# Feature arrays held twice, the staging array dropped, and the packs issued in slots 10 to 12

## What is computed

```python
f = b[:, :, ::2, ::2]                                   # 40 x 40 features
w = extract_patches(f, 3, 1)                            # 1600 patches of 64*3*3
wn = w / max(norm(w), 1e-4)
yi = einsum('bpd,bld->blp', w, wn) * mm                 # 1600 x 1600 scores
yi = softmax(yi * 10, axis=1) * mm
patches = einsum('blp,bld->bpd', yi, raw_w)             # raw_w: 4 x 4 patches of b
out = overlap_add(patches) / 4
```

## Time and profile before

| | us |
|---|---|
| median of three runs | 1486.64 (1485.1 to 1486.96) |
| the profiled execution | 1485.93 |
| its span | 1484.1 |

### The profile page before, as it was taken

How to read it: one execution, slowest core, us unless ns; L and a number is a source line. 1 busy time by engine, 2 the same in 40 slices (tenths; PEclk the granted TensorE clock), 3 DMA queues, 4 the chain that set the end, 5 groups by cost and what they waited for, 6 DMA issues and landing times.

```text
span 1484.1 us, 24228 instructions
## 1 busy us (share of the span) xinstructions
PE 1340.5 (90%) x7190; PEld 904.1 (61%) x7190; DVE 1195.3 (81%) x2830; ACT 853.7 (58%) x2233; POOL 47.6 (3%) x63
## 2 busy tenths in 40 slices
PE   4987999989999799998999899998999989999796
PEld 4765755667556675576656576566755666557343
DVE  4667889779888798878897878977888879888883
ACT  2667646656457564585555754666655755458431
POOL 1000000010000100001000000000000010000100
PEclk9997999999999999999999999999999999999999
DMA  5305462155622744137631556215462255412442
GB/s 101 45 1 133 108 130 70 51 150 116 127 61 65 172 101 109 52 85 165 122 93 34 130 128 136 78 44 143 119 124 72 62 143 113 111 51 83 129 137 57
DMA packets 181749, 146.57 MB, mean 99 GB/s; under 512 B 120114, under 2 KB 177522, under 8 KB 181618
## 3 DMA queue, kind: packets, MB, share of 16 engines
q1 hardware_dynamic: 181298, 144.04, 41.0%
q10 hardware_dynamic: 320, 0.99, 0.3%
HBM read 19.76 MB, written 13.11 MB: 22 GB/s over the span
## 4 chain that ended last, share of the span: by engine, by line
PE 32%; DVE 28%; SPq 11%; ACT 11%; issue 10%; DMA 7%; DVEq 0%; POOL 0%; ACTq 0%; POOLq 0%
PE psG L465 14%; PE psO L515 14%; DVE G L934 7%; DVE Z L967 5%; DVE G L874 4%; SPq L318 4%; DVE S L880 4%; DVE G L945 4%; ACT S L690 3%; ACT G L701 3%; SPq L299 3%; DMA HV<-LOHI 3%; PE psG L474 3%; ACT G L676 3%; DMA SH<-G 3%
## 5 line engine op out<-in xcount | busy, mean ns | idle before, releaser
L515 PE MATMUL psO<-Z,B 123*128 123x492 f32 (+2 forms) x1792 | 718.4, 530 | 38.5 <-DVE Z L967 25.2
L515 PEld LDWEIGHTS psO<-Z,B 123*128 123x128 f32 x1792 | 326.4, 194 | 238.1 <-issue 129.9
L465 PE MATMUL psG<-LH,HL 128*123 128x246 f16 (+2 forms) x2616 | 411.8, 287 | 38.2 <-DMA HV<-LOHI 28.7
L465 PEld LDWEIGHTS psG<-LH,HL 128*123 128x123 f16 x2616 | 280.5, 139 | 161.0 <-issue 96.7
L880 DVE CUSTOM_DVE_ANT_0 S<-G,RB 123x492 f32<-123x492 f32 (+1 forms) x448 | 269.1, 607 | 87.4 <-DVE G L874 55.0
L701 ACT ACTIVATE G<-G,nb 123x492 f32<-123x492 f32 (+1 forms) x448 | 267.0, 642 | 110.9 <-DVE G L934 110.4
L690 ACT ACTIVATE S<-S,nm 123x480 f32<-123x480 f32 (+3 forms) x560 | 307.3, 555 | 2.3 <-DVE nm L885 2.1
L945 DVE TENSOR_TENSOR G<-G,SH 123x492 f32<-123x492 f32 (+1 forms) x448 | 247.3, 591 | 54.2 <-DMA SH<-G 53.9
L934 DVE SCALAR_TENSOR_TENSOR G<-G,RA,psB 123x492 f32<-123x492 f32 (+1 forms) x448 | 270.1, 646 | 0.5 <-issue 0.5
L676 ACT ACTIVATE G<-psG 123x492 f32<-123x492 f32 (+3 forms) x256 | 120.1, 472 | 173.0 <-PE psG L465 92.5
L967 DVE TENSOR_TENSOR Z<-G 123x984 f32<-123x984 f32 (+2 forms) x192 | 197.3, 1028 | 0.6 <-PE psO L515 0.6
(11 more groups left out here) (83 smaller groups left out, 581.3 us busy)
## 6 DMA issues: line engine op xcount, KB each, us to landing
SH<-G SPq DMA_DIRECT2D x336, 214.8 KB
SH<-G SPq DMA_DIRECT2D x112, 89.2 KB
SH<-G SPq DMA_DIRECT2D x336, 19.2 KB
XP<-x SPq DMA_DIRECT2D x20, 280.0 KB, 5.9
XP<-mid SPq DMA_DIRECT2D x20, 280.0 KB, 5.3
HL<-LOHI SPq DMA_DIRECT2D x16, 246.5 KB, 3.5
mid<-OSB SPq DMA_DIRECT2D x48, 80.0 KB, 2.3
out<-OSB SPq DMA_DIRECT2D x48, 80.0 KB, 2.3
```

What stands on the lines that cost most here:

```text
L465: last = pe.matmul(psG[0:TW, bank, b0 * TW:b1 * TW], st[:, p:p + TW], mv[:, lo:lo + n], start=i == 0, stop=i == len(terms) - 1)
L515: last = pe.matmul(psO[:, b, 0:n], B[:, o:o + 128], Z[:, 2 * (s % 2) + j, 0:n], start=t == 0, stop=t == TILES - 1)
```

## The change

LH, HL, H1 and HV become two buffers each; unit w uses buffer w % 2. The staging array goes: `high_features` and `low_features` write straight into LH of the unit's buffer, whose two halves are the low and the high part. So the two LH packs go, and six are left (`N_F` = 6). They are issued in slots 10 (HL), 11 (H1) and 12 (HV), two each, behind the slot's copies, instead of all in slot 28 ahead of them. SP's wait for all scores of v in slot 28 becomes, in each of the three slots and for w of 2 and more, a wait for the scores of unit w - 2, which are long done. `high_features` waits for the same instead of for `f_in`. At the start DVE clears LH (twice the size) and no longer HL, H1 and HV, POOL no longer clears LOHI, and ACT's queue issues only the two HV packs.

```diff
-        HL = sb("HL", [128, FLEN], F16)
-        LH = sb("LH", [128, FLEN], F16)
-        H1 = sb("H1", [128, FLEN], F16)
-        HV = sb("HV", [128, FLEN], F16)
+        LH = sb("LH", [128, 2, FLEN], F16)
+        HL = sb("HL", [128, 2, FLEN], F16)
+        H1 = sb("H1", [128, 2, FLEN], F16)
+        HV = sb("HV", [128, 2, FLEN], F16)
-        LOHI = sb("LOHI", [128, FLEN], F16)
-        LS, HS = LOHI[0:64, :], LOHI[64:128, :]
-        CLEARED = 10
+        CLEARED = 6
-        N_F = 8
+        N_F = 6
+        def halves_of(w):
+            return LH[0:64, w % 2, :], LH[64:128, w % 2, :]
...
             def lay_out_features(w, which):
+                if w >= 2:
+                    sp.wait_ge(g_ready, (w - 1) * NB)
+                    sp.sem_inc(sp_gate, 1)
                 sp.wait_ge(h_made, 2 * (w + 1))
                 sp.sem_inc(sp_gate, 1)
                 sp.wait_ge(l_made, 2 * (w + 1))
-                for dst, src in packs(which):
+                for dst, src in packs(w, which):
                     sp.dma_start(dst, src).then_inc(f_in, 16)
...
-                    if s == SLOTS and w is not None:
-                        sp.wait_ge(g_ready, (v + 1) * NB)
-                        sp.sem_inc(sp_gate, 1)
-                        lay_out_features(w, ("HL", "LH", "H1", "HV"))
                     at = place(u, v, s + LEAD)
                     if at:
                         shift_pair(at)
                     at = place(u, v, s + 2)
                     if at and at[2] == 0:
                         shift_strip(at)
+                    if s in (10, 11, 12) and w is not None:
+                        lay_out_features(w, (("HL", "H1", "HV")[s - 10],))
...
-            def high_features(v, w):
+            def high_features(w):
                 act.wait_ge(feat_in, (w + 1) * STRIPS * 16)
-                if v is not None:
+                if w >= 2:
                     act.sem_inc(act_gate, 1)
-                    act.wait_ge(f_in, (v + 1) * N_F * 16)
+                    act.wait_ge(g_ready, (w - 1) * NB)
+                HS = halves_of(w)[1]
...
-            for tile, value in ((HL[:, :].bitcast(F32), 0.0), (LH[:, :].bitcast(F32), 0.0), (H1[:, :].bitcast(F32), 0.0),
-                                (HV[:, :].bitcast(F32), 0.0), (halves[0:64, 0:1], 1.0), ...
+            for tile, value in ((LH[:, :, :].bitcast(F32), 0.0), (halves[0:64, 0:1], 1.0), ...
...
-            pool.memset(LOHI[:, :].bitcast(F32), 0.0).then_inc(cleared, 1)
```

More of the change, by code:

```diff
@@ L244, in out_parts, with packs @@
                         yield a, j, at[0] - first, len(at), rows[at[0]] - 1 + a
-        def packs(which):
+        def halves_of(w):
+            return LH[0:64, w % 2, :], LH[64:128, w % 2, :]
+        def packs(w, which):
             n = FLEN
-            parts = {"HL": ((HL[0:64, :], HS), (HL[64:128, :], LS)), "LH": ((LH[0:64, :], LS), (LH[64:128, :], HS)),
-                     "H1": ((H1[0:64, :], HS), (H1[64:128, 0:n - 1], HS[:, 1:n])),
-                     "HV": ((HV[0:64, :], HS), (HV[64:128, 0:n - TW], HS[:, TW:n]))}
+            low, high = halves_of(w)
+            hl, h1, hv = (a[:, w % 2, :] for a in (HL, H1, HV))
+            parts = {"HL": ((hl[0:64, :], high), (hl[64:128, :], low)),
+                     "H1": ((h1[0:64, :], high), (h1[64:128, 0:n - 1], high[:, 1:n])),
+                     "HV": ((hv[0:64, :], high), (hv[64:128, 0:n - TW], high[:, TW:n]))}
             return [part for name in which for part in parts[name]]
@@ L457, in one_row, with products @@
                 return [(HL, LH, dy, dx) for dx in range(3)] + [(H1, H1, dy, 0), (HL, HL, dy, 2)]
-            def products(j, par, bank, b0, b1, terms):
+            def products(v, j, par, bank, b0, b1, terms):
                 s0 = S_CHUNKS[j // PAIRS][0]
@@ L464, in products @@
                     lo, p = (s0 + b0 + dy) * TW + dx, (t + dy) * TW + dx
-                    last = pe.matmul(psG[0:TW, bank, b0 * TW:b1 * TW], st[:, p:p + TW], mv[:, lo:lo + n],
+                    last = pe.matmul(psG[0:TW, bank, b0 * TW:b1 * TW], st[:, v % 2, p:p + TW], mv[:, v % 2, lo:lo + n],
                                      start=i == 0, stop=i == len(terms) - 1)
@@ L480, in even_tile @@
                     pe.wait_ge(p_copied, v * len(SHARED) + count(SHARED, j) - 1)
-                    products(j, 0, FREE, stored, w, SHARED_ROWS).then_inc(p_ready, 1)
+                    products(v, j, 0, FREE, stored, w, SHARED_ROWS).then_inc(p_ready, 1)
                 pe.wait_ge(even_read, v * SLOTS + j + 1)
@@ L488, in even_tile @@
                 if shared:
-                    last = products(j, 0, 0, stored, w, one_row(0))
+                    last = products(v, j, 0, 0, stored, w, one_row(0))
                 last.then_inc(g_ready, 1)
@@ L497, in odd_tile @@
                 if alone > stored:
-                    products(j, 1, 1, stored, alone, TERMS)
+                    products(v, j, 1, 1, stored, alone, TERMS)
                 if alone < w:
-                    last = products(j, 1, 1, alone, w, one_row(2))
+                    last = products(v, j, 1, 1, alone, w, one_row(2))
                 last.then_inc(g_ready, 1)
@@ L765, in body @@
                         if s == 5:
-                            high_features(v, w)
+                            high_features(w)
                         if s == 6:
@@ L778, in _ @@
             act.wait_ge(cleared, CLEARED)
-            high_features(None, 0)
+            high_features(0)
             squares(0)
@@ L783, in _ @@
             act.wait_ge(l_made, 2)
-            for dst, src in packs(("LH", "HV")):
+            for dst, src in packs(0, ("HV",)):
                 act.dma_start(dst, src).then_inc(f_in, 16)
@@ L802, in _ @@
             dve.sem_inc(dve_gate, 1)
-            for tile, value in ((HL[:, :].bitcast(F32), 0.0), (LH[:, :].bitcast(F32), 0.0), (H1[:, :].bitcast(F32), 0.0),
-                                (HV[:, :].bitcast(F32), 0.0), (halves[0:64, 0:1], 1.0), (halves[64:128, 1:2], 1.0), (SH[:, :, :], 0.0), (SHJ[:, :], 0.0)):
+            for tile, value in ((LH[:, :, :].bitcast(F32), 0.0), (halves[0:64, 0:1], 1.0), (halves[64:128, 1:2], 1.0), (SH[:, :, :], 0.0), (SHJ[:, :], 0.0)):
                 dve.memset(tile, value).then_inc(cleared, 1)
@@ L809, in low_features @@
             def low_features(w):
+                LS, HS = halves_of(w)
                 dve.wait_ge(h_inner, w + 1)
```

## The result

The changed kernel takes **1448.37 us** in the median of four runs (1442.97 to 1450.82), beside 1486.8 before: a ratio of 0.9737, with a 95% interval of 0.9704 to 0.977. Five later runs of it (e11), beside the kernel before on the same chip, gave 1449.4 and 0.976 (0.9736 to 0.9784). The forecast was 1452, and the range held it. The profiled execution took 1450.82 us with a span of 1449.0; by the sum of the prediction it should have been 1451.0.

The account below looks back on a forecast made before the run. No engine alone sets the time; the loop argument, exponential, shifted copy, add, Z, paste does, with the scores woven in. Boundary idle 34.0 plus start 0.9 gives 34.9 us off: 1451.7, say 1452 us, range 1444 to 1464.

Parts of the forecast that it names:

- DVE's idle at the boundary: At seven body boundaries, slot 2: DVE's waits for copies and odd score tile go, 34.0 us in all.
- the case that the prediction kept as its lower end: PE's scores at half clock behind the boundary: 4.16 us of DVE's idle goes instead of 5.06; 1457 us.
- The granted clock stays at 1.00 across the boundary: Sign in the new trace: PE's clock no longer falls to 0.50 behind its paste.
- The start: PE's wait for unit 0's packs goes, six landing earlier than eight: 0.9 us, bounds 0 and 0.9.
- The packs in slots 10 to 12: Six bodies: pack issues fit SP's free time, copies still land in time; cost 0, bounds 0 and 14 us.
- The upper bound of 14 us: Cost if a pair of packs holds slot 12's strip copy: 2.3 us in each of six bodies.
- SP's backlog: Boundary: place 5's copies and the store move ahead 4 us or more, keeping their distance to DVE; nothing counted.
- Rival (a): Boundary: place 4's copies stay late, DVE keeps its first wait; gain 23 us, 1463.5; chance 0.18 with part of slots' cost.
- Rival (b): Behind the boundary PE sets the pace: gain its stall plus lost clock, 47 us, 1439 us; chance 0.10.
- Rival (c): Slots 10 to 13: SP becomes the bound, packs hold the copies; 77 us lost, 1529 us; chance 0.06.
- Rival (d): Boundary: PE's next wait, for Z from DVE, is just as late; within 0.2% of 1486.6 us; chance 0.04.
- the two LH packs at 0: Slot 28: dropping them (1.70 us of SP, 493 KB) from a stretch already emptied gains 0.

Follow-up runs that it names:

- e11: The changed kernel itself, unedited, in five later runs beside the kernel before on the same chip; 1449.4 us (0.976).
- e1: Changed kernel with only the packs' place undone: all six issued in slot 28 ahead of the shift copies; 1459.59 us (ratio to before 0.9807).
- e5: Changed kernel with all packs of units 2 to 7 left out, so part of the computation is changed; 1451.43 us (0.977).
- e6: Changed kernel with all six packs in slot 10, ahead of that slot's copies; 1463.23 us (0.9849).
- e2: Changed kernel with eight spare pack-sized copies to HBM, issued by SP in slot 28 ahead of the shift copies; 1462.58 us (0.9832).
- e3: Changed kernel with one more wait of PE at slot 2, for DVE's argument of slot 2; 1474.49 us (0.9913).
- e4: Changed kernel with image DMAs spread, two behind the copies of each of slots 9, 10 and 11, packs moved to slots 12 to 14; 1437.53 us (0.9666).
- e8: Changed kernel with 632 of 7190 PE matmuls cut, which changes the scores; 1432.76 us (0.9638).
- e9: Kernel with the spread image load (e4), with 632 of 7190 PE matmuls cut; 1396.91 us (0.9396).
- e7: Kernel before, single buffers and staging array kept, with only the two LH packs of units 1 to 7 left out; 1464.75 us (0.9862).

## Why the prediction was right, step by step

*DVE's idle at the boundary, 34.0 us.* Right in sum (34.0 between the marks) and in mechanism: at the fifth boundary both waits are gone, and only the 0.63 us three slots on is new. That the sum is right to the tenth is luck: 31.1 us of it are fewer waits of DVE and 2.7 us less busy time, and the errors of the bodies cancel. It was right less well one by one: 4.9, 5.4, 5.4, 3.9, 5.1, 5.6 and 3.7 were forecast, 3.0, 5.3, 6.0, 2.4, 5.5, 5.7 and 6.2 came. The first fell short by the clock, the case that the prediction kept as its lower end. There PE waits 2.97 us for Z, a gap that e1 and e5 have as well, and the window 138 to 142 is granted half the clock; DVE then waits for the odd tile (timeline, window, waits from 134 to 154):

```profile
137.00 5.29 PE L521 MATMUL psO<-Z,B 123*128 123x369 f32 x8 [2.97 <-DVE Z L974]
```

```profile
138.00:142.00 4.00, 4.00 (x7) 2.02 (x7) 3.97 (x9) 1.50 (x4) 0.92 (x1) 0.50 0.43 134
```

```profile
DVE G L881 <- ACT G L683: 1.5, 1, 1.5
```

"The granted clock stays at 1.00 across the boundary" was thus right for five of seven boundaries in this execution: at the second, too, a gap of 2.13 us was followed by the lower clock (paste in 4.38 instead of 2.75 us). At 1001 us a gap of 2.12 us was not. The profile of e11, another execution of the same kernel, shows that this is not fixed by the kernel. Its first boundary has the same gap of 2.97 us, but the clock came back sooner and DVE didn't wait:

```profile
137.52 4.19 PE L521 MATMUL psO<-Z,B 123*128 123x369 f32 x8 [2.97 <-DVE Z L974]
```

Its second has a gap of 2.12 us and 1.00 behind it, and its bodies win 5.1, 6.0, 5.7, 4.6, 4.5, 5.3 and 5.6 us over the same profile of before, 36.8 together. So the short gains of the first and the fourth body belong to one execution. In the fourth, DVE's waits show where it went: 3.9 us are gone at the boundary, but those for strip copies grew from 1.1 to 2.2 us, those at slot 11 by 0.5 and that for ACT's small result (df<-ed) by 0.5. The last body won more than forecast in both profiles, because the forecast had only DVE's two large waits there (3.7 us) and left out 1.0 us for ACT's result (L914), which went too. That the clock makes the spread of the runs is likely, since the execution of 1442.97 us had a mean clock of 0.99 and the slowest two 0.985 and 0.986, but no run tests it.

*The start, 0.9 us.* 1.6 us came: PE's first scores start at 27.72 instead of 28.86, 1.1 us earlier, and the rest came by slot 28. The bound of 0.88 was drawn at the end of the work before, as the profile modelled it; the first matmul starts before that end.

*The packs in slots 10 to 12, 0 us.* Right, by e5. The issuing was sized too high: 1.15 + 1.14 + 1.13 = 3.4 us instead of 5.3, since the rows of before have the price behind other packs. The cover that was named, two slots between copy and use, is the true one: without it (e6) the packs cost 12 to 15 us. The upper bound of 14 us had another mechanism, a held strip copy; the waits of e6 are for the shift copies.

*SP's backlog, nothing on top.* Nearly right as a sum. That SP "keeps its distance to DVE" was not: SP moved ahead by 3 to 4 us and DVE by 5.3, and the waits at slot 5, 2.9 us in all, are new. By e2 the backlog is worth 14 us by itself, and it would come due mostly there, at slot 5, not at slot 2.

*Rival (a), copies of place 4 late:* did not happen, though 1.3 us of margin was all there was. *Rival (b), PE the bound:* wrong for the boundary, by e2, where PE has no added gap and the time follows DVE's waits (in e3 both engines lose, so it can't tell them apart), but less wrong than its 0.10 for the slots behind it. The argument against it, that the chain runs through DVE there, doesn't hold: e4, e8 and e9 show two engines that are both full, of which the chain names one. A gain at the boundary larger than what PE gained (4.16 us and the clock) might have been cut as in e4; no run tests that. *Rival (c):* excluded by e5. *Rival (d):* PE's wait for Z was indeed next, and earlier than the packs.

What the prediction didn't see is how the gain is made up. It treated the stall as one piece that goes with the packs' place, and put the two LH packs at 0 because the stretch is already emptied. By e7, 21 of the 38 us come from the two LH packs that are no longer made, and by e1, 11 from the new place behind that; the 6 us between lie in the start, in the end behind the last mark and in the spread of the runs. The forecast of the sum doesn't depend on this split, but the one for the place alone does: the 23 us expected in e1 were twice too much.

## What to carry to other kernels

A stall's price is what the engine that carries the chain idles, not what the stalled engine does; read it there, and then look at the stalled engine's clock behind the gap, because here the fall of the clock cost more than the gap itself (0.6 to 0.8 us without it, 3.5 to 4.8 with it and a gap under 1 us longer). Transfers that nobody waits for soon are free only behind the ones that are waited for, a few per slot: the same packs cost nothing in three slots behind the copies and 12 to 15 us in one block ahead of them, and spreading the image load in the same way won 11 us. Where two engines are both full, a wait taken from one pays only as far as the other allows; cutting the other's work in a trial run shows how far that is.

## What the runs showed of the hardware

Whether the lower clock level follows a gap is not a matter of the gap's length alone. Single gaps of 2.5 to 2.95 us were followed by 1.00 five times in e1, but the gap of 2.13 us at the second boundary of the changed kernel was not, and one of 2.12 us at the same place in e11 was. The length of two gaps in a row doesn't settle it either: 2.20 and 2.12 us with one paste between them were followed by the lower clock in e1 (0.57 in the window), 2.17 and 2.12 us with the same paste by 1.00 in e7. Every gap of 3.4 us or more at a boundary was followed by it, seven times in e3 and six times in the kernel before.

Issuing a DMA costs SP more right behind others: the two HV packs took 2.51 us to issue as the last of eight, 1.97 us as the last of six in e1, and 1.13 us alone in slot 12.
